# Two fused layers on one Trainium2 core: weight pieces loaded early, shared blocks nearer to their tiles, routing cut into steps

## The chip, the cores and the metric

The kernel runs on one core of one Trainium2 chip. The time is the device time of one execution in microseconds (us); lower is better. In the profile PE is TensorE (PEld its weight loads), DVE is VectorE, ACT is ScalarE, POOL is GpSimd and SP is SyncE, which here only issues DMAs.

## What is computed

The input `x` is 2048 rows (4 batches of 512) of 512 channels. There are two layers, each `x = x + ffn(cond(x))`:

- `cond` gates x with a two-way exponential scan over time. Per batch and channel, with decay d, it runs a = a*d + exp(k)*v and b = b*d + exp(k) forwards and backwards; the output is sigmoid(x) * num / den, scaled per batch. k and v are the side input, so the scans do not depend on x.
- `ffn` of layer 0: an rms norm, then 8 experts (512 to 256 to 512 with silu(g)*u), the 2 best for each row, plus one shared expert for all rows.
- `ffn` of layer 1: 32 experts (512 to 352 to 512), the 6 best for each row with softmax weights, plus a shared expert of width 704, which the kernel treats as two experts of 352.

```
x = x + ffn0(cond0(x));  x = x + ffn1(cond1(x))
y[t] = sum over the top k experts e of w[t,e] * (silu(x W1[e]) * (x W3[e])) W2[e];  plus the shared expert
```

## The kernel before

The rows are cut into 16 tiles of 128. Work for the experts is done in *blocks* of 128 rows by one expert. Blocks are numbered through: 0 to 15 are shared blocks of layer 0, 16 to 54 (`R0` = 16, 39 blocks) routed blocks of layer 0, 55 to 86 (`S1` = 55) the 32 shared blocks of layer 1 (two per tile, experts 32 and 33), and 87 to 214 (`R1` = 87, 128 blocks) its routed blocks. A routed block first gathers its rows by an indirect DMA.

A block has these steps. `gu_pe` (L1749) multiplies the tile by gate and up weights: in layer 1, 24 matmuls, since each weight and each x is held as a high and a low float16 half. `gu` is a tanh on ACT (L1187) and two products on DVE (L1574, L1576). `h_turn` transposes on PE (L1766), ACT copies (L1200), DVE makes the low half (L1584). `down` (L1798) is the second product.

**Weights.** They come as `PIECES` of 128 x 1088 float32 (544 KB) in layer 1, four per expert; pieces 27 to 30 are shared expert 32, 31 to 34 expert 33, 35 to 50 experts 0 to 3. A piece goes through one of two staging buffers `ST`: `w_load` (SP, L923) loads it, `w_hi` (ACT, L1168, and L1172 for pieces whose low half is made by POOL) makes the high half, `w_lo` (DVE L1555 or POOL L975) the low half. A load waits until the low half of the piece two before it is made. `AHEAD` names pieces that are loaded to free parts of the weight buffers and so need no staging buffer; the others are the `RING`.

**Order of the work.** The generator `stages()` yields (step, number) pairs. Every engine walks the same list and takes the steps it has a part in, so the list is the order of each engine's queue, and of SP's and POOL's too. Waits are on semaphores.

**Around the change.** The layer 0 routed loop runs over `j` from 0 to 41; block R0+j starts in step j and ends in step j+3. Its 27 spare steps also carry halves of the scans (`k_...`, DVE L1285 to L1321). Then come two `pick`s (POOL, L1035: each gathers two sets of rows of layer 0's expert output), four splits of weights (`weights(4, 51)`), `x_sum` (DVE, L1341) and a tanh. Then a loop over `s` from 0 to 17 prepares tile s of layer 1: `gate` (DVE, L1332), `f_hi` (ACT, L1131), `f_lo` (DVE, L1358), `row` and `x_turn` (SP: a store, and a DMA transpose, L907), `f_turn` and `logit` (PE L1640 and L1651, ACT L1138, DVE L1370) of the tile before, and `x_sum`, tanh of the tile after. `f_hi` of a tile waits until the transpose of the tile before has landed. Each s has two half steps (slots) `slot = 2s + h`, and each slot runs one shared block:

```
for h in (0, 1):
    b = 2 * (s - 3) + h
    slot = 2 * s + h
```

so the blocks of tile s run at s + 3. At the end of each s one weight piece (two while s < 4) is loaded and split.

**Routing** of layer 1 goes by groups of four tiles (g = 0 to 3). At s = 4g+4, h = 1: `r_top` (DVE: `max` and `max_index` of four tiles L1384 and L1385, L1387, L1392, the one-hot L1393, the sum L1398) and `r_red` (L1404, L1408 or L1410). At s = 4g+5, h = 1: `r_pos` (PE, L1670 to L1674), `r_copy` (DVE L1439), `r_wts` (L1416 to L1431) and `r_slot` (L1445 to L1454, with `split_slot` L1457 to L1461). Then the 24 `hot` steps (DVE L1471, L1475, with PE L1685), six per group. After s = 17 a tail written by hand holds hots 18 to 23, shared blocks 30 and 31, `table1` (L1484, L1486), the first gathers (L1003), and the routed blocks follow.

Of the kernel before, what the change touches and what calls it, by code (L numbers as in the profile page):

```python
# [11 lines left out]
F32 = mybir.dt.float32  # L12
# [80 lines left out]

AHEAD = (17, 18, 19, 20)
RING = [k for k in range(len(PIECES)) if k not in AHEAD]


# [15 lines left out]
def stages():  # L115
# [276 lines left out]
    for j in range(NB0 + 3):  # L392
        n = R0 + j
        if n + 3 < S1:
            yield "gather", n + 3
        if n + 2 < S1:
            yield "x_turn", n + 2
        if n < S1:
            yield "gu_pe", n
        yield from turn_made()  # L400
        if j * 27 // 39 != (j - 1) * 27 // 39 or j >= 39:
            yield from next_half()
        if n - 1 < S1:
            yield "h_turn", n - 1
        if n < S1:
            yield "gu", n
        yield from after_half()
        if n - 2 < S1:
            yield "h_low", n - 2
        if 1 <= j:  # L410
            yield "down", n - 3
        if 37 <= j < 41:
            yield "y_load", j - 37
    while half[0] < 64:
        yield from next_half()
        yield from after_half()
    yield from turn_made()
    for i in range(2):
        yield "pick", i
    yield from weights(4, 51)  # L420
    yield "x_sum", 0
    yield "f_tanh", NT

# [5 lines left out]
    for s in range(18):  # L429
        f = NT + s  # L430
        if 1 <= s <= NT:
            yield "f_turn", f - 1
        if s < NT:
            yield "gate", f
            yield "f_hi", f
            yield "f_lo", f
            yield "row", f
            yield "x_turn", S1 + s
        if s + 2 < NT:
            yield "pick", s + 2  # L440
        if s < 8:
            yield "k_back", s + 8
        for h in (0, 1):
            b = 2 * (s - 3) + h
            slot = 2 * s + h
            yield from shared(b, "gu_pe")
            yield from shared(b - 1, "h_turn")
            yield from shared(b, "gu")
            if h == 1 and s % 4 == 1 and s > 1:
                yield "r_pos", 4 + s // 4 - 1  # L450
                yield "r_copy", 4 + s // 4 - 1
            elif h == 1 and 1 <= s <= NT:
                yield "logit", f - 1
            for g in range(3):
                if 0 <= slot - 1 - 2 * (4 * g + 6) < 6:
                    yield "hot_pe", 6 * g + slot - 1 - 2 * (4 * g + 6)
            yield from shared(b - 2, "down")
            if h == 1 and s % 4 == 1 and 1 < s <= NT:
                yield "logit", f - 1
            if h == 0 and 4 <= s + 2 < NT:  # L460
                yield "y_load", s + 2
            if h == 1 and s + 1 < NT:
                yield "x_sum", s + 1
                yield "f_tanh", f + 1
            for g in range(4):
                if h == 1 and s == 4 * g + 4:
                    yield "r_top", 4 + g
                    yield "r_red", 4 + g
                if h == 1 and s == 4 * g + 5:
                    yield "r_wts", 4 + g  # L470
                    yield "r_slot", g
                if g < 3 and 0 <= slot - 2 * (4 * g + 6) < 6:
                    yield "hot", 6 * g + slot - 2 * (4 * g + 6)
        yield from weights(2 if s < 4 else 1, 51)

    for q in range(18, 21):
        yield "hot", q
# [68 lines left out]
def build(nc, xtok, fT, cst, svec, cond, rout, gatew, W0, W1, Y1):  # L546
    with ExitStack() as ctx:
# [111 lines left out]
        d_pick = [sem(f"d_pick{i}") for i in range(2)]  # L659
        d_first = sem("d_first")  # L660
        d_w = [sem(f"d_w{i}") for i in range(2)]
        d_ahead = sem("d_ahead")
        d_g = [sem(f"d_g{i}") for i in range(3)]
        d_t = [sem(f"d_t{i}") for i in range(4)]
        d_row = [sem(f"d_row{i}") for i in range(6)]
# [55 lines left out]
        def staged(k):  # L721

            l, e, c0, cw, at, who = PIECES[k]
            if k in AHEAD:
                m = AHEAD.index(k)
                to = 18432 + 3072 * (m // 2)
                return (Whi, Wlo)[m % 2][:, to:to + 2 * cw].bitcast(F32), d_ahead, 16 * (m + 1)
            m = RING.index(k)
            return ST[m % 2][:, 0:cw], d_w[m % 2], 16 * (m // 2 + 1)

# [104 lines left out]
        def _(eng):  # L835
# [82 lines left out]
            def w_load(k):  # L918
                l, e, c0, cw, at, who = PIECES[k]
                if k not in AHEAD and k >= 2:  # L920
                    eng.wait_ge(*low(RING[RING.index(k) - 2]))
                at, there, count = staged(k)
                S.dma_start(at, WD[l][e][:, c0:c0 + cw]).then_inc(there, 16)  # L923

# [121 lines left out]
        def _(eng):  # L1046
# [101 lines left out]
            def w_hi_(k):  # L1148
# [3 lines left out]
                eng.wait_ge(there, count)  # L1152
                if k == 21:

                    for j in AHEAD[-2:]:
                        eng.wait_ge(*low(j))
                if spare(k) is not None:
                    eng.wait_ge(b_down, spare(k) + 1)
# [73 lines left out]
        def _(eng):  # L1232
# [128 lines left out]
            def logit(f):  # L1361
                l, i = tile(f)
                E = EXPERTS[l]
                eng.wait_ge(f_lgm, f + 1)
                if l == 0:

                    eng.wait_ge(f_pow, f + 1)
                    V.tensor_scalar(lg[:, i % 4, 0:E], l_bank[l][:, 0:E], sm[:, f, 2:3], None, ALU.mult).then_inc(f_lg, 1)
                else:
                    V.tensor_copy(lg[:, i % 4, 0:E], l_bank[l][:, 0:E]).then_inc(f_lg, 1)  # L1370

            def choices(l, b):

# [4 lines left out]
            def r_top(g):  # L1378
# [1 line left out]
                E, K_ = EXPERTS[l], TOPK[l]  # L1380
                o, ot = choices(l, b)
                eng.wait_ge(f_lg, 4 * g + 4)
                for q in range(4):
                    after(V.max(mx[:, q, :], lg[:, q, 0:E]))  # L1384
                    after(V.max_index(ix[:, q, :], mx[:, q, :], lg[:, q, 0:E]))  # L1385
                m0 = mx[:, :, 0:1]
                op = V.tensor_tensor(ex[:, :, 0:E], lg[:, :, 0:E], bc(m0, [P, 4, E]), ALU.subtract)  # L1387
                if l == 1:
# [1 line left out]
                if l == 0:  # L1390
                    V.tensor_tensor(et[:, :, 0:K_], mx[:, :, 0:K_], bc(m0, [P, 4, K_]), ALU.subtract).then_inc(r_sub, 1)
                after(V.tensor_copy(ixf[:, :, 0:K_], ix[:, :, 0:K_]))  # L1392
                after(V.tensor_tensor(o, bc(iota[:, 0:E].unsqueeze(1).unsqueeze(1), [P, 4, K_, E]),  # L1393
                                      bc(ixf[:, :, 0:K_].unsqueeze(3), [P, 4, K_, E]), ALU.is_equal))

                if g >= 1:
                    eng.wait_ge(r_pos, g)
# [43 lines left out]
            def r_slot(b):  # L1441
# [4 lines left out]
                                                [P, 4, K_, E]), ALU.mult))  # L1446
                ks = slice(0, 4 * K_)
                after(V.tensor_reduce(gq[:, ks].rearrange("p (q k) -> p q k", q=4), ot, AX_X, ALU.add))
                split_slot(ks)
                after(V.scalar_tensor_tensor(out=ja[:, ks].rearrange("p (q k) -> p q k", q=4), in0=ixf[:, :, 0:K_],  # L1450
                                             scalar=4.0, in1=gj[:, ks].rearrange("p (q k) -> p q k", q=4),
# [11 lines left out]
            def hots(h):  # L1463
# [3 lines left out]
                    eng.wait_ge(r_tab, 1 + h - 1)  # L1467
                else:
                    eng.wait_ge(b_down, S1)
                n0 = 4 * h % 24  # L1470
                V.tensor_tensor(A16, bc(iota16[:, :].unsqueeze(1), [P, 4, P]),  # L1471
                                bc(qa[:, n0:n0 + 4].unsqueeze(2), [P, 4, P]), ALU.is_equal)
# [113 lines left out]
            def down(n):  # L1586
                what, l, j = kind(n)
                o, first, last = finished(n)
                if what == "routed" or l == 0 or not last:
# [5 lines left out]
                                       op0=ALU.mult, op1=ALU.add).then_inc(b_outv, 1)  # L1595

            mine = dict(setup=setup, k_min=k_min_, k_fwd=k_fwd, k_bwd=k_bwd, k_den=k_den_, k_rec=k_rec_,
                        k_out=k_out_, x_sum=x_sum, gate=gate, f_var=f_var_, f_lo=f_lo_, logit=logit, r_top=r_top, r_red=r_red_,
                        r_wts=r_wts, r_copy=r_copy, r_slot=r_slot, hot=hot, places0=places0, table0=table0, table1=table1, w_lo=w_lo, weight=weight, gu=gu,
                        h_turn=h_turn, down=down)  # L1600
            for what, n in stages():
                if what in mine:
# [263 lines left out]
```

## Time and profile before

| | us |
|---|---|
| median of 3 runs | 1608.49 (1602.04 to 1611.96) |
| profiled execution, its own time | 1601.73 |
| its span | 1599.6 |
| PE busy | 1342.6 (84%) |
| DVE busy | 1006.1 (63%) |
| ACT, POOL busy | 742.2, 604.6 |

Times within the profile are counted from the start of the span. Busy times are of instructions; PE's matmuls are pipelined, so their single durations overlap. PEclk is the clock granted to TensorE as a share of full speed. In a timeline row, the bracket gives how long the engine was idle before the row and what ended that.

### The profile page before, as it was taken

What the parts mean: (1) busy time and instruction counts of PE and PEld (TensorE: products, weight loads), DVE (VectorE), ACT (ScalarE), POOL (GpSimd) and SP (SyncE); (2) the same over time, 40 slices, a digit from 0 to 9 for tenths busy, and PEclk for the clock granted to TensorE, in tenths of its full rate; (3) what the DMA queues carried; (4) which work ended last, traced back from release to release, by engine and by line L of the source; (5) the groups of instructions that cost most, each with busy time, mean ns of one, the idle gap of its engine ahead of it and who ended that gap; (6) DMA issues with size and microseconds to landing.
All of it is one profiled execution on the core that took longest, in us unless ns stands there. A gap on an engine that the chain in (4) does not pass through costs nothing.

```text
span 1599.6 us, 23683 instructions
## 1 busy us (share of the span) xinstructions
PE 1342.6 (84%) x8220; PEld 811.3 (51%) x8220; DVE 1006.1 (63%) x1748; ACT 742.2 (46%) x1262; POOL 604.6 (38%) x466
## 2 busy tenths in 40 slices
PE   0146666699997289889899999999999999999998
PEld 0023342244443156556565666666666666666664
DVE  8999978979896468888735444444444444444222
ACT  4466664545454543333146454454444445444332
POOL 2344432544431443231033443444444444444443
PEclk9987766899999599999999999999999999999999
DMA  3557644689985896563048988889998988988664
GB/s 101 174 174 187 156 112 92 151 182 195 206 177 159 227 205 145 141 146 83 25 137 233 203 199 212 196 207 199 207 208 195 206 203 204 200 206 184 109 115 74
DMA packets 225234, 269.38 MB, mean 168 GB/s; under 512 B 149664, under 2 KB 149792, under 8 KB 224992
## 3 DMA queue, kind: packets, MB, share of 16 engines
q1 hardware_dynamic: 188464, 175.84, 42.6%
q0 software_dynamic: 36656, 92.03, 29.2%
q8 instruction: 70, 1.15, 0.3%
q14 instruction: 44, 0.36, 0.1%
HBM read 167.87 MB, written 70.32 MB: 149 GB/s over the span
## 4 chain that ended last, share of the span: by engine, by line
PE 60%; DVE 26%; issue 5%; DMA 4%; ACT 3%; POOL 1%; SPq 0%; POOLq 0%; ACTq 0%; DVEq 0%
PE psG L1749 33%; PE psO L1798 19%; DVE wkFD L1314 5%; PE psH L1766 3%; DMA ST<-W 2%; DVE wkFN L1289 2%; DVE wkFD L1296 2%; PE psX L1710 2%; DVE wkFD L1285 2%; DMA XSp<-XG 2%; DVE wkFN L1321 1%; DVE wkFD L1306 1%; DVE H L1574 1%; DVE Wlo L1555 1%; DVE wkFN L1299 1%
## 5 line engine op out<-in xcount | busy, mean ns | idle before, releaser
L1749 PE MATMUL psG<-Whi,XSp 128*128 128x352 f16 (+2 forms) x3000 | 671.8, 329 | 12.1 <-issue 10.8
L1749 PEld LDWEIGHTS psG<-Whi,XSp 128*128 128x128 f16 x3000 | 295.7, 100 | 212.5 <-issue 38.4
L1798 PE MATMUL psO<-Whi,HS 128*128 128x512 f16 (+1 forms) x1180 | 394.5, 387 | 0.0
L1749 PE MATMUL psG<-Wlo,XSp 128*128 128x352 f16 (+2 forms) x1500 | 389.2, 329 | 0.0
L1021 POOL DMA_INDIRECT out<-OB,posb x128 | 202.7, 1583 | 416.1 <-ACT OB L1222 407.5
L1555 DVE SCALAR_TENSOR_TENSOR Wlo<-ST,Whi 128x1088 f16<-128x1088 f32 (+1 forms) x118 | 152.3, 1291 | 235.4 <-ACT Whi L1168 231.4
L1574 DVE SCALAR_TENSOR_TENSOR H<-H,psG 128x352 f32<-128x352 f32 (+1 forms) x215 | 105.5, 491 | 242.2 <-ACT H L1187 221.4
L1798 PE MATMUL psO<-Wlo,HS 128*128 128x512 f16 (+1 forms) x590 | 228.4, 387 | 0.0
L1187 ACT ACTIVATE H<-psG 128x352 f32<-128x352 f32 (+1 forms) x215 | 95.2, 443 | 229.7 <-PE psG L1749 222.5
L1749 PEld LDWEIGHTS psG<-Wlo,XSp 128*128 128x128 f16 x1500 | 149.1, 99 | 93.4 <-issue 8.3
L1798 PEld LDWEIGHTS psO<-Whi,HS 128*128 128x128 f16 x1180 | 117.6, 100 | 120.4 <-issue 9.8
L1222 ACT ACTIVATE OB<-psO,WSL 128x512 f32<-128x512 f32 x128 | 88.1, 688 | 173.7 <-PE psO L1798 173.7
L1003 POOL DMA_INDIRECT XG<-xrows,posb x128 | 129.5, 1012 | 90.9 <-DVE posb L1486 42.4
L1168 ACT ACTIVATE Whi<-ST 128x1088 f16<-128x1088 f32 (+1 forms) x118 | 129.7, 1100 | 28.1 <-DMA ST<-W 28.1
L975 POOL TENSOR_TENSOR Wlo<-ST,Whi 128x1088 f16<-128x1088 f32 (+1 forms) x37 | 82.0, 2218 | 154.6 <-ACT Whi L1172 154.5
L1576 DVE SCALAR_TENSOR_TENSOR H<-H,psG 128x352 f32<-128x352 f32 (+1 forms) x215 | 106.4, 495 | 7.4
L1200 ACT CAST HS<-psH 128x384 f16<-128x384 f32 x160 | 75.7, 473 | 71.9 <-PE psH L1766 71.9
L963 POOL TENSOR_TENSOR wkFN<-wkFN,wkEU 128x512 f32<-128x512 f32 x32 | 40.5, 1267 | 180.6 <-DVE wkEK L1276 169.5
L1314 DVE RECIPROCAL wkFD<-wkFD 128x512 f32<-128x512 f32 x32 | 107.1, 3346 | 0.0
L1620 PE MATMUL psX<-C,wkFN 128*128 128x128 f32 x64 | 16.7, 412 | 101.9 <-DVE wkFN L1321 101.9
L1584 DVE TENSOR_TENSOR HS<-psH,HS 128x384 f16<-128x384 f32 x160 | 88.1, 551 | 16.2 <-ACT HS L1200 16.2
L1766 PE MATMUL psH<-C,H 128*128 128x128 f32 x480 | 80.5, 277 | 19.3 <-DVE H L1576 19.3
(216 smaller groups left out, 1536.9 us busy)
## 6 DMA issues: line engine op xcount, KB each, us to landing
ST<-W SPq DMA_DIRECT2D x136, 544.0 KB
ST<-W SPq DMA_DIRECT2D x23, 512.0 KB
slots<-OB SPq DMA_DIRECT2D x39, 256.0 KB
wkK<-fT SPq DMA_DIRECT2D x32, 256.0 KB
xrows<-XG SPq DMA_DIRECT2D x20, 256.0 KB, 4.4
y0rows<-x SPq DMA_DIRECT2D x8, 512.0 KB, 5.5
y0rows<-OB POOLq DMA_DIRECT2D x16, 256.0 KB, 4.3
out<-OB SPq DMA_DIRECT2D x16, 256.0 KB
```

Source lines behind the costliest of these rows:

```text
L1003: G.indirect_dma_start(out=XG[g % 3][:, 0:w], out_offset=None, in_=X[l][:, :], in_offset=bass.IndirectOffsetOnAxis(ap=idx[l][:, j:j + 1], ...
L1021: G.indirect_dma_start(out=Y1[:, :], out_offset=bass.IndirectOffsetOnAxis(ap=idx[1][:, j:j + 1], axis=0), in_=OB[o % 4][:, :], in_offset=N ...
L1168: op = A.activation(st if who == "pool" else hi, st, ACT.Copy, scale=WS)
L1187: A.activation(H32[a][:, 0:F], psG[a][0][:, 0:F], ACT.Tanh, scale=0.5 * UN).then_inc(b_tanh, 1)
L1222: A.activation(OB[o % 4][:, :], psO[bank(o)][:, :], ACT.Copy, scale=scale).then_inc(b_outa, 1)
L1314: V.reciprocal(FD[n % 2][:, :], FD[n % 2][:, :]).then_inc(k_rec, 1)
L1555: op = V.scalar_tensor_tensor(out=Wlo[:, at:at + cw], in0=st, scalar=WS, in1=Whi[:, at:at + cw], op0=ALU.mult, op1=ALU.subtract)
L1574: V.scalar_tensor_tensor(out=H, in0=H, scalar=1.0, in1=g, op0=ALU.add, op1=ALU.mult).then_inc(b_sil, 1)
L1576: V.scalar_tensor_tensor(out=H, in0=H, scalar=(-0.5, 0.5)[l] * XS * UN * UN, in1=u, op0=ALU.mult, op1=ALU.mult).then_inc(b_h, 1)
L1749: op = M.matmul(o, hx[:, x, q * P:q * P + P], w(half_, off + c, nn), start=first, stop=last)
L1766: op = M.transpose(bank_[:, q * P:q * P + P], H32[a][:, q * P:q * P + P], ident)
L1798: op = M.matmul(psO[bank(o)][:, :], hs(n)[:, x, q * P:q * P + P], columns[n](half_, off0 + q * 512, 512), start=(q == 0 and x == 0 and hal ...
```

## The change

It has three parts. (1) Pieces 29 and 30 join `AHEAD`; pieces 27 and 28 are loaded to the two staging buffers at j = 20 of the layer 0 routed loop, 29 and 30 at j = 22 and 24, to bytes of the weight buffers that the layer 0 shared expert had. After the loop come the four `y_load`s (moved there from j = 37 to 40), the splits of 27 and 28, the two picks, the loads of 31 and 32, and the splits of 29 and 30. Each piece in `AHEAD` has a semaphore of its own. (2) A shared block b runs in slot b + 4 instead of b + 6, for b up to 27; blocks 28 and 29 run in slots 33 and 35, where 32 and 34 have none. The tail is unchanged. (3) Layer 1's routing: `max` and `max_index` of each tile directly after its logits; the sum over the one-hot (`r_mask`) and `r_red` half a stage later; `r_wts` and the second part of `r_slot` (`r_place`) half a stage after the first part.

```
-AHEAD = (17, 18, 19, 20)
+AHEAD = (17, 18, 19, 20, 29, 30)
...
-        if 37 <= j < 41:
-            yield "y_load", j - 37
+        if j == 20:
+            yield from loads(2, 51)
+        if j in (22, 24):
+            yield "w_load", 29 + (j - 22) // 2
...
     yield from turn_made()
+    for i in range(4):
+        yield "y_load", i
+    yield from splits(2)
     for i in range(2):
         yield "pick", i
-    yield from weights(4, 51)
+    yield from loads(2, 51)
+    yield from splits(2)
...
-            b = 2 * (s - 3) + h
             slot = 2 * s + h
+            b = slot - 4 if slot < 32 else {33: 28, 35: 29}.get(slot, -9)
...
                 if h == 1 and s == 4 * g + 4:
                     yield "r_top", 4 + g
+                if h == 0 and s == 4 * g + 5:
+                    yield "r_mask", 4 + g
                     yield "r_red", 4 + g
                 if h == 1 and s == 4 * g + 5:
+                    yield "r_slot", g
+                if h == 0 and s == 4 * g + 6:
                     yield "r_wts", 4 + g
-                    yield "r_slot", g
+                    yield "r_place", g
...
+    yield "r_wts", 7
+    yield "r_place", 3
...
             def w_load(k):
...
+                if k in AHEAD and l == 1:
+
+                    eng.wait_ge(b_down, R0)
...
             def logit(f):
...
+                    eng.wait_ge(f_lg, f + 1)
+                    largest(i % 4, E)
+
+            def largest(q, E):
+                after(V.max(mx[:, q, :], lg[:, q, 0:E]))
+                after(V.max_index(ix[:, q, :], mx[:, q, :], lg[:, q, 0:E]))
...
+            def r_place(b):
+                K_ = TOPK[1]
+                ks = slice(0, 4 * K_)
                 split_slot(ks)
```

The first hots and the high half of piece 47 also wait for the low halves of pieces 29 and 30, whose staging bytes they overwrite.

## Rows read from the trace of the kernel before

**Rows 1.** Busy time by stretch: us, then each engine's busy time, PEclk, DMA share, GB/s.
```profile
556.10:591.90 35.80, 33.65 (x207) 21.41 (x205) 20.90 (x42) 18.13 (x26) 15.51 (x9) 0.93 0.97 206
...
556.10:807.40 251.30, 224.98 (x1483) 143.63 (x1481) 188.05 (x429) 84.11 (x141) 64.35 (x42) 0.96 0.52 126
...
591.90:653.70 61.80, 56.32 (x375) 36.30 (x372) 49.97 (x111) 21.80 (x37) 18.11 (x13) 0.97 0.65 153
653.70:715.30 61.60, 55.58 (x374) 36.16 (x374) 49.99 (x111) 21.79 (x37) 18.14 (x13) 0.97 0.57 140
715.30:777.00 61.70, 56.28 (x391) 36.81 (x392) 46.67 (x109) 19.21 (x35) 9.20 (x6) 0.97 0.26 76
777.00:807.40 30.40, 23.16 (x141) 12.96 (x140) 20.52 (x61) 3.18 (x6) 3.39 (x4) 0.89 0.17 54
...
890.00:1600.00 710.00, 701.77 (x4612) 439.24 (x4610) 305.47 (x555) 323.72 (x501) 299.99 (x230) 1.00 0.84 185
```
**Rows 2.** Who PE waited for, 556 to 815: us in total, times, longest.
```profile
PE psH L1766 <- DVE H L1576: 19.3, 9, 4.2
```
**Rows 3.** DVE's timeline in two groups: start us, us, engine, line, instruction.
```profile
584.73 0.19 DVE L1384 MAX8 mx<-lg 128x8 f32<-128x32 f32 x1
...
586.83 0.29 DVE L1387 TENSOR_TENSOR ex<-lg,mx 128x128 f32<-128x128 f32 x1
...
588.24 1.51 DVE L1398 TENSOR_REDUCE mask<-OH 128x128 f16<-128x768 f32 x1
...
590.19 1.76 DVE L1408 COPY macc<-mred 128x32 f16<-128x32 f16 x1
591.87 0.68 DVE L1332 SCALAR_TENSOR_TENSOR XR<-XR,RT 128x512 f32<-128x512 f32 x1
...
602.12 0.28 DVE L1416 TENSOR_REDUCE s<-ex 128x4 f32<-128x128 f32 x1
...
605.16 2.20 DVE L1457 CAST gi<-gq 128x24 int32<-128x24 f32 x1
...
608.68 0.69 DVE L1332 SCALAR_TENSOR_TENSOR XG<-XG,RT 128x512 f32<-128x512 f32 x1
```
**Rows 4.** DVE's timeline, the gates of tiles 7, 8 and 9.
```profile
619.77 0.68 DVE L1332 SCALAR_TENSOR_TENSOR XG<-XG,RT 128x512 f32<-128x512 f32 x1
...
633.17 0.68 DVE L1332 SCALAR_TENSOR_TENSOR XR<-XR,RT 128x512 f32<-128x512 f32 x1
...
653.72 0.68 DVE L1332 SCALAR_TENSOR_TENSOR XR<-XR,RT 128x512 f32<-128x512 f32 x1
```
**Rows 5.** Timeline of all engines between the layers, 512 to 557.
```profile
512.93 0.60 ACT L1222 ACTIVATE OB<-psO 128x512 f32<-128x512 f32 x1 [0.70 <-PE psO L1798]
...
517.98 0.97 POOL L1035 DMA_INDIRECT wkFD<-slots,sl  x1 [14.76 <-DMA slots<-OB]
...
519.50 1.11 ACT L1168 ACTIVATE Whi<-ST 128x1088 f16<-128x1088 f32 x1 [5.97 <-DMA ST<-W]
...
523.18 2.24 POOL L975 TENSOR_TENSOR Wlo<-ST,Whi 128x1088 f16<-128x1088 f32 x1 [0.43 <-ACT Whi L1172]
...
531.87 2.30 DVE L1332 SCALAR_TENSOR_TENSOR XG<-XG,RT 128x512 f32<-128x512 f32 x1 [1.99 <-ACT XG L1108]
...
543.87 1.09 PE L1640 MATMUL psX<-C,XG 128*128 128x128 f32 x4 [0.62 <-issue]
...
556.11 0.80 PE L1749 MATMUL psG<-Whi,XSp 128*128 128x352 f16 x2
```
**Rows 6.** The picks (L1035), 505 to 760: from issue to landing.
```profile
DMA to landing us min/median/max: 3.5/5.4/10.6
```
**Rows 7.** The chain of waits, 440 to 900: start us, us, what.
```profile
514.39 6.45 DMA ST<-W
```
**Rows 8.** The layer 0 routed loop, 340 to 505: busy by stretch.
```profile
340.00:505.00 165.00, 154.56 (x767) 75.98 (x765) 147.70 (x174) 87.20 (x198) 61.73 (x54) 1.00 0.84 188
```
**Rows 9.** The layer 0 routed loop: who waited for whom.
```profile
PE psG L1749 <- DMA XSp<-XG: 0.7, 1, 0.7
```

More of the change, by code:

```diff
@@ L661, in build @@
         d_w = [sem(f"d_w{i}") for i in range(2)]
-        d_ahead = sem("d_ahead")
+        d_ahead = [sem(f"d_ahead{i}") for i in range(6)]
         d_g = [sem(f"d_g{i}") for i in range(3)]
@@ L726, in staged @@
                 to = 18432 + 3072 * (m // 2)
-                return (Whi, Wlo)[m % 2][:, to:to + 2 * cw].bitcast(F32), d_ahead, 16 * (m + 1)
+                return (Whi, Wlo)[m % 2][:, to:to + 2 * cw].bitcast(F32), d_ahead[m], 16
             m = RING.index(k)
@@ L1153, in w_hi_ @@
                 if k == 21:
-                    for j in AHEAD[-2:]:
+                    for j in AHEAD[2:4]:
+                        eng.wait_ge(*low(j))
+                if k == 27 + 4 * 5:
+                    for j in AHEAD[4:]:
                         eng.wait_ge(*low(j))
@@ L1382, in r_top @@
                 eng.wait_ge(f_lg, 4 * g + 4)
-                for q in range(4):
-                    after(V.max(mx[:, q, :], lg[:, q, 0:E]))
-                    after(V.max_index(ix[:, q, :], mx[:, q, :], lg[:, q, 0:E]))
+                if l == 0:
+                    for q in range(4):
+                        largest(q, E)
                 m0 = mx[:, :, 0:1]
@@ L1394, in r_top, with r_mask_ @@
                                       bc(ixf[:, :, 0:K_].unsqueeze(3), [P, 4, K_, E]), ALU.is_equal))
+                if l == 0:
+                    r_mask_(g)
+            def r_mask_(g):
+                l, b = divmod(g, 4)
+                E = EXPERTS[l]
+                o, ot = choices(l, b)
                 if g >= 1:
@@ L1469, in hots @@
                     eng.wait_ge(b_down, S1)
+                    for j in AHEAD[4:]:
+                        eng.wait_ge(*low(j))
                 n0 = 4 * h % 24
@@ L1597, in _ @@
             mine = dict(setup=setup, k_min=k_min_, k_fwd=k_fwd, k_bwd=k_bwd, k_den=k_den_, k_rec=k_rec_,
-                        k_out=k_out_, x_sum=x_sum, gate=gate, f_var=f_var_, f_lo=f_lo_, logit=logit, r_top=r_top, r_red=r_red_,
-                        r_wts=r_wts, r_copy=r_copy, r_slot=r_slot, hot=hot, places0=places0, table0=table0, table1=table1, w_lo=w_lo, weight=weight, gu=gu,
+                        k_out=k_out_, x_sum=x_sum, gate=gate, f_var=f_var_, f_lo=f_lo_, logit=logit, r_top=r_top, r_red=r_red_, r_mask=r_mask_,
+                        r_wts=r_wts, r_copy=r_copy, r_slot=r_slot, r_place=r_place, hot=hot, places0=places0, table0=table0, table1=table1, w_lo=w_lo, weight=weight, gu=gu,
                         h_turn=h_turn, down=down)
```

## The prediction

> **What bounds the kernel now.** I read the busy time by stretch first, then PE's waits, then the timelines of single engines. From 890 us to the end PE is busy 701.8 of 710 us at full clock [rows 1]: the routed blocks of layer 1 run at PE's pace, and the change does not touch them. So whatever is won before 807.40, when the first routed block starts, should come through to the end unchanged, unless the weight loads behind it depend on the clock time; they don't, they are issued in the order of the list.
>
> The change acts on three places. (a) Between the layers: the last output of layer 0 is made at 512.93 and the first shared block of layer 1 starts at 556.11 [rows 5]; in these 43 us PE does little. (b) The shared stage, 556.10 to 807.40: PE is busy 225.0 of 251.3 us, so 26.3 are idle: 2.2 up to 591.9, then 5.5, 6.0 and 5.4 in three groups of about 61.7, and 7.2 in the tail [rows 1]. 19.3 us of waits on this stage are one kind: PE's transpose waiting for DVE's product [rows 2]. (c) The layer 0 routed loop, into which loads are put: PE busy 154.6 and DVE 147.7 of 165 us, the DMA engines 84% [rows 8].
>
> Why PE waits for DVE is seen in DVE's timeline. At the end of one stage in four DVE does `r_top` and `r_red` in one go from 584.73 to 591.87, 7.1 us, and one stage later `r_wts` and `r_slot` from 602.12 to 608.68, 6.6 us [rows 3]. Behind them in its queue stand the gate, the low half and the products of the next block. A stage without them takes 633.17 - 619.77 = 13.4 us, the one that ends in `r_top` 653.72 - 633.17 = 20.55 [rows 4]. The granted clock falls with it: 0.97 over each group [rows 1].
>
> **Part 1, loads ahead and splits first.** Now ACT ends the last output at 512.93 + 0.60 = 513.5 and starts splitting piece 27 at 519.50, since its load was only issued then; the gate of tile 0 runs from 531.87 to 534.17, 2.30 long where others take 0.68 [rows 4, 5]. After the change pieces 27 and 28 lie in their buffers, so by ACT durations of 1.11 us:
> - ACT: 27 to 514.7, 28 (two passes) to 516.9; POOL's low half, 2.24 [rows 5], to 519.2.
> - POOL's queue: the picks now stand behind that low half and start at 519.2 instead of 517.98. So the edit costs the picks 1.2. The second gather of pick 0 is issued 1.3 later, 520.5, and lands 5.4 later (median, 3.5 to 10.6) [rows 6]: 525.9.
> - DVE: two sums of 0.75 (L1341), tanh 0.6 (ACT L1108), gate 0.7: the gate ends at about 528.7, against 534.17. That is 5.5 earlier. DVE no longer has the low half of 29 ahead of `x_sum`, and the gate does not meet POOL's low half.
>
> The `y_load`s go from inside the loop to behind the last store on SP, some 2 us of issues that land before the picks: nothing. From the gate on, the steps of tiles 0 and 1 are the same and in the same order, with the same loads beside them (eight pieces split before s = 2 in both), so PE's transpose of tile 1 goes from 543.87 [rows 5] to about 538.4.
>
> **Part 2, blocks two slots earlier.** `gu_pe` of the first shared block now stands right behind that transpose (1.1 us): 539.5 instead of 556.11, 16.6 earlier. Its weights 27 to 30 are split long before. Block 1 needs piece 34, whose low half is the last of s = 1, about 546; block 0 at the low clock takes 6 to 7 us, so PE waits about 1. At s = 2 and 3 ACT still has two pieces per stage to split ahead of the tanh of a block, and PE, which had no blocks at s = 2, will now wait there once, about 2. The low clock at the start costs as before plus about 2.5, since PE did less before. Start-up extra: 5.5.
>
> **Part 3, routing in steps.** The work stays: DVE is busy 50.0 of 61.8 us in a group [rows 1], which includes all of it. What goes is the block of 7.1 and that of 6.6. They become, per slot: 0.53 per tile after its logits, 1.4 (L1387 to L1393), 2.1 to 3.6 (L1398 to L1408), 1.9 (L1445, L1448), 1.1 + 3.5 (`r_wts`, `r_place`) [rows 3]. A slot of PE is 6.7 us; DVE's own work in one is 3.8 to 4.1 and a hot 1.5. So the worst slots have 5.6 + 1.5 = 7.1 and 5.3 + 4.6 = 9.9, against 6.7 and a slack of about 3, the time that PE spends on `down` and the next `gu_pe` before it needs the products. Nearly all of it fits: I leave 1.5 us of idle per group instead of 5.5 to 6.0, and give back 1.2 per group for the clock. Bounds: nothing left (0) and nothing won (5.6).
>
> The row L1408 copies 32 columns in 1.76 us, as the cast L1457 of 24 columns takes 2.20 [rows 3]; each ends with a POOL low half that it met. The Trainium skill (SBUF — State Buffer, "SBUF: two separate sides") says that DVE and GpSimd share a port pair by an exclusive lock that is held for the whole instruction. By that rule cutting the routing into steps cannot remove these meetings, only move them. The trace agrees, and the 1.1 us (L1408) and 2.0 us (L1457) are kept in the slots above.
>
> **The loads in the layer 0 loop.** Four pieces more. Lower bound nothing: in 165 us PE waited 0.7 us for a transpose [rows 9], and one is issued two blocks before its use. Upper bound: the whole time to the landing of a piece in a crowd, 6.45 [rows 7], for each of four: 26. Nearest is the slack row, so 1. PE and DVE are both near full here, so nothing is gained either. The Trainium skill (DMA: Bandwidth & Descriptors, "Queues, rings and completion order") says that each DMA engine takes the descriptors of one ring in order. By this a transpose issued by SP just after the pieces waits for them, which speaks against the change; no row here shows such a pair. It would take the cost from 1 towards the upper bound, and is the rival below.
>
> **The sum.** 539.5 + PE's work 225.0 - 3 x 1.2 (clock) + idle outside the groups 2.2 + 7.2 + groups 3 x 1.5 + start-up 5.5 = 780.3, against 807.4: 27.1. The tail: the last group's routing chain (logit 31 to `r_place`) now has blocks 28 and 29 over it instead of 26 to 29. Counted through from the logits it needs about 13.4 us to hot 18 while PE has 18 of work to the end of block 31, so it is covered; I allow 1.1. Minus 1 for the loop: gain 25. Span 1574.6, own time 1576.7. The profiled execution lies 6.8 below the median of the three runs (1608.49); against that median, 1583.5. I forecast 1583.5 us.
>
> **The rivals.**
> - *DVE becomes the bound of the shared stage.* DVE would be busy 50 of some 56 us, and the slot with `r_wts`, `r_place`, a hot and a POOL meeting is over budget. If the groups keep 4 to 5.5 of idle and the low clock, 8 to 15 of the gain go: 1592 to 1600, middle 1594. For it: the 9.9 us slot. Against: the stages with hots alone run at 13.4, with PE full.
> - *The start moves, not the blocks.* The first block is early, but then waits: picks that land after 10.6 [rows 6] and transposes that hold `f_hi` up, so that only the 5.5 and part of the 11 remain. Gain 16 to 18: 1591. Against: from s = 2 on the tiles have 13 us per stage, and need 8.
> - *More than forecast.* Nothing remains of the groups' idle and the start costs nothing extra: 4.5 + 4 + 1.1 more, gain 35: 1573.
> - *Slower: transposes behind the pieces in the layer 0 loop.* Place: j = 20 to 24. If each piece holds a transpose back past its slack, DVE, which carries the scans there, and PE both stop, up to 26 [rows 7]; with the next gather, that waits for the transpose, doubling it, up to 40 or more. It decides from 25 us, over 6 per piece: 1608 to 1625, at its middle 1612. Against: the 0.7 us of rows 9.
> - *That the change does nothing* would need the first block to start where it did; it stands two slots earlier in PE's list and its weights are there, so 2 in 100.
>
> **How the numbers follow.** A measurement of this kernel tells about 1%, 16 us, from no change. Forecast (gain 18 to 32) 0.60; DVE bound 0.15; start only 0.09; more than forecast 0.08; slower 0.05; nothing 0.03. Faster by over 1%: forecast, more, a fifth of the DVE case and over half of the start case, 0.60 + 0.08 + 0.04 + 0.06 = 0.78. Slower by over 1%: part of its case and unknowns, 0.04. Within 1%: 0.18. The range takes in gains of 12 to 38: 1570 to 1597.
>
> **What would show it.** Right: the first PE row of L1749 in layer 1 near 539 to 541 and a first routed block near 782; the gate of tile 0 at 0.7 us; stages of 13.4 to 14.5 us throughout, PE idle under 2 in each group and PEclk 0.99 or 1.00 there; PE's wait for L1576 under 8 us instead of 19.3; the stretch from the first routed block to the end unchanged at 792. Wrong: a last layer 0 output later than 515 (the loads hurt), PE in the groups waiting for L1576 in the slot after `r_place`, or gates still 15 us apart.

## The result, and the profile after

| | kernel before | changed kernel |
|---|---|---|
| median, us | 1603.95 (1600.6 to 1611.96, 20 runs) | 1599.03 (1594.6 to 1602.0, 20 runs) |
| profiled execution: own time, span | 1601.73, 1599.6 | 1600.68, 1598.8 |
| first shared block, first routed block of layer 1 | 556.11, 807.40 | 541.69, 804.94 |

The ratio is 0.9963 [0.9951, 0.9975]: 5 to 6 us faster (the medians are 4.9 apart), where 25 were forecast (1583.5, range 1570 to 1597). The gain is clear of noise and under 1%. The forecast's ratio against its own median was 0.984. That median, 1608.49 of 3 runs, lies 4.5 above the one of 20 runs here, so the gain misses its forecast by some 20 us, while the time misses it by 15.5 only.

The busy time by stretch of the changed kernel: the shared stage, its start, its three groups, its tail, the routed blocks. The columns are those of [rows 1].

```profile
541.70:804.90 263.20, 231.83 (x1493) 147.18 (x1492) 188.69 (x433) 88.23 (x147) 68.47 (x46) 0.94 0.59 131
541.70:592.70 51.00, 44.46 (x253) 27.70 (x252) 25.80 (x50) 22.21 (x34) 18.52 (x12) 0.87 0.86 194
592.70:651.80 59.10, 55.45 (x382) 36.68 (x381) 48.54 (x111) 22.02 (x38) 17.73 (x12) 1.00 0.77 168
651.80:710.70 58.90, 54.35 (x376) 35.72 (x375) 48.74 (x111) 21.71 (x38) 17.70 (x12) 1.00 0.71 147
710.70:771.00 60.30, 50.92 (x315) 31.72 (x313) 43.10 (x101) 18.26 (x32) 11.17 (x6) 0.89 0.31 72
771.00:804.90 33.90, 26.65 (x175) 15.37 (x174) 22.51 (x64) 4.03 (x8) 3.35 (x4) 0.90 0.16 48
890.00:1598.00 708.00, 700.44 (x4602) 438.16 (x4600) 305.40 (x555) 323.77 (x501) 299.44 (x230) 1.00 0.85 185
```

The shared stage starts 14.4 us earlier and is 11.9 longer (263.2 against 251.3), so 2.5 remain at the first routed block. From there to the end it is 793.9 us, against 792.2. Over all the profiles of this case that stretch takes 792.2 to 795.0, so the end carries through what is won before it, as assumed, but only to within some 3 us. The three groups are 59.1, 58.9 and 60.3 long instead of 61.7, 6.8 us less together, where the prediction's three groups of 1.5 idle and a 1.2 repayment for the clock stood for about 16. (The third group isn't the same work: the shift leaves it 315 matmuls instead of 391.)

Who PE waited for, 537 to 815, in the changed kernel (us in total, times, longest):

```profile
PE psO L1724 <- DVE Whi L1514: 7.9, 5, 2.1
PE psH L1805 <- DVE H L1615: 7.9, 6, 2.2
PE psX L1690 <- ACT HT L1154: 6.0, 1, 6.0
PE psO L1724 <- DVE Wlo L1514: 5.9, 3, 3.4
PE psX L1709 <- DVE mask L1430: 4.2, 3, 1.5
```

The 19.3 us for H [rows 2] are 7.9. But PE now waits 13.8 us for the selectors of `hot` (L1514; 3.1 in the kernel before) and 4.2 for the mask, for which it did not wait before. Between the layers and at the start of the stage (timeline of the changed kernel; start us, us, engine, line, instruction, idle before it and its releaser):

```profile
514.31 0.60 ACT L1241 ACTIVATE OB<-psO 128x512 f32<-128x512 f32 x1 [0.70 <-PE psO L1837]
514.80 1.10 ACT L1187 ACTIVATE Whi<-ST 128x1088 f16<-128x1088 f32 x1
...
520.50 1.85 POOL L1051 DMA_INDIRECT wkFD<-slots,sl  x1
...
526.12 2.26 POOL L991 TENSOR_TENSOR Wlo<-Wlo,Whi 128x1088 f16<-128x1088 f32 x1
526.37 2.57 DVE L1360 SCALAR_TENSOR_TENSOR wkK<-wkFD,wk,wkK 128x512 f32<-128x512 f32 x1 [4.86 <-DMA wkFN<-slots,sl]
528.97 0.75 DVE L1360 SCALAR_TENSOR_TENSOR wkK<-wkFN,wk,wkK 128x512 f32<-128x512 f32 x1
...
530.41 0.69 DVE L1351 SCALAR_TENSOR_TENSOR XG<-XG,RT 128x512 f32<-128x512 f32 x1 [0.70 <-ACT XG L1124]
...
541.69 0.79 PE L1788 MATMUL psG<-Whi,XSp 128*128 128x352 f16 x2
...
549.07 0.46 PE L1788 MATMUL psG<-Whi,XSp 128*128 128x352 f16 x2 [1.92 <-POOL Wlo L991]
```

Against [rows 5]: ACT splits piece 27 right behind the last output, the first gate ends at 531.10 instead of 534.17, and the first shared block stands right behind the transpose of tile 1. The stages, from gate to gate of tiles 0 to 15 (each the difference of two such L1332 or L1351 rows), show where the time went again:

```
before   8.0 8.2  9.1 13.4 21.2 16.8 11.1 13.4 20.6 16.7 11.0 13.4 20.5 16.6 11.0   sum 211.1
changed  6.4 8.9 14.1 15.9 17.0 15.5 15.4 13.4 14.8 15.3 15.3 13.4 14.8 16.9 16.7   sum 213.8
```

The stages of tiles 2 and 3, which now hold the early blocks, went from 22.5 to 30.0 us; and at the other end, slot 32 holds no `gu_pe` any more, so PE has nothing between the last `down` and the selectors of `hot`:

```profile
754.77 2.11 DVE Wlo L1510
...
757.83 0.61 PE L1724 MATMUL psO<-Wlo 128*128 128x128 f16 x4 [3.41 <-DVE Wlo L1514]
...
758.23 0.79 PE L1788 MATMUL psG<-Whi,XSp 128*128 128x352 f16 x2
...
764.17 0.46 PE L1788 MATMUL psG<-Whi,XSp 128*128 128x352 f16 x2
```

(The first line is of the chain of waits, the others of the timeline.) PE waits 3.41 us and comes back at 0.79 us for a pair of matmuls instead of 0.46, the lower of its two levels, for most of block 28.

### The profile page after: what moved, and what is told of

Its sections match the earlier page's. It is cut to its first block, busy times and chain, and to the rows that moved or that the text cites. A ratio compares the mean times of both kernels' runs of the same rounds, so it can differ in the third digit from the quotient of the medians.

```text
span 1598.8 us, 23690 instructions
## 1 busy us (share of the span) xinstructions
PE 1345.1 (84%) x8220; PEld 811.5 (51%) x8220; DVE 1003.3 (63%) x1748; ACT 740.8 (46%) x1262; POOL 602.0 (38%) x466
## 4 chain that ended last, share of the span: by engine, by line
PE 59%; DVE 25%; issue 7%; ACT 4%; DMA 4%; POOL 1%; SPq 0%; POOLq 0%; ACTq 0%; DVEq 0%
PE psG L1788 33%; PE psO L1837 19%; DVE wkFD L1333 5%; PE psH L1805 3%; DMA ST<-W 2%; DVE wkFN L1308 2%; DVE wkFD L1304 2%; PE psX L1749 2%; DVE wkFD L1315 2%; DMA XSp<-XG 1%; DVE wkFN L1340 1%; DVE wkFD L1325 1%; DVE H L1613 1%; DVE XG L1377 1%; DVE Wlo L1594 1%
## 5 line engine op out<-in xcount | busy, mean ns | idle before, releaser
L1659 PE MATMUL psX<-C,wkFN 128*128 128x128 f32 x64 | 16.6, 411 | 101.5 <-DVE wkFN L1340 101.5
L1623 DVE TENSOR_TENSOR HS<-psH,HS 128x384 f16<-128x384 f32 x160 | 88.1, 550 | 15.5 <-ACT HS L1219 14.9
```

## The experiments

The expectations name their theories by letters, and A does not mean the same in all of them. For `only_loads` and `only_steps`, A is the prediction's sum taken part by part. For `only_shift`, A says that an earlier first block counts (10 to 12 us), and C that the shift only lengthens the stages it enters and leaves the emptied slots slow (0 to 4 us). In `late_shift`, what C said is called A. Theory D, on record with the first runs and tested by the later ones, says that cutting up the bursts turns PE's waits for H into waits for `hot` and the mask. All ratios are to the kernel before, run on the same chip beside them.

**The parts alone.** `only_loads` is the kernel before with the early loads and splits (the `AHEAD`, `loads`, `splits` and `w_load` edits), `only_steps` with the step routing (`r_mask`, `r_place`, `largest`), and `only_shift` with one line (and a separate semaphore for each `AHEAD` piece, as in the changed kernel):

```diff
-            b = 2 * (s - 3) + h
             slot = 2 * s + h
+            b = slot - 4 if slot < 32 else {33: 28, 35: 29}.get(slot, -9)
```

`only_loads`. Expected:

> Part 1 alone (pieces 27 to 30 loaded ahead, splits before the picks, y_loads after the loop); blocks and routing as before. Theory A (each part gives what the sum said, the loss is in the others): the start gains its 3 to 5 us and all of it comes through to the end: 1600 us, 3 to 4 below the kernel before. Theory B (the loads cost the layer 0 loop what they give the start): within 2 us of the kernel before; the last layer 0 output is 1.4 us later in the trace.

`only_shift`. Expected:

> Part 2 alone (shared blocks two slots earlier, none in slots 32 and 34). Theory A (PE is the bound of the shared stage, so an earlier first block counts): 10 to 12 us faster. Theory C (the stage is paced by DVE's and ACT's queue, tile by tile, so blocks that are two slots nearer only make the stage s = 2 longer and leave PE idle and slow in the empty slots): 0 to 4 us faster, the gate of the last tile 4 to 6 us later than before, PE waiting for the hots at slot 32.

`only_steps`. Expected:

> Part 3 alone (routing in steps). Theory A: PE's waits for DVE's products go from 19 us to under 8 and nothing takes their place: 13 to 16 us faster. Theory D (the wait moves: PE's hot_pe waits for the hot that now stands behind r_wts and r_place, and r_pos for the mask): 4 to 8 us faster, with 5 us or more of PE waits on the hots (L1471/L1475 by the old numbers) and 3 us on the mask.

`no_steps`, the loads and the shift together. Expected:

> Parts 1 and 2 without part 3. If the parts add up, this lies above the changed kernel by what only_steps gains. Theory A: 13 to 16 us above it, 1613. Theory C and D: 4 to 8 us above it, 1603 to 1607, that is about the kernel before.

| kernel | median, us | ratio |
|---|---|---|
| only_loads | 1600.16 | 0.9964 [0.9947, 0.9982] |
| only_shift | 1610.27 | 1.0022 [0.9998, 1.0045] |
| only_steps | 1600.18 | 0.9969 [0.9954, 0.9985] |
| no_steps (loads and shift) | 1605.47 | 0.9997 [0.9979, 1.0014] |

The loads are worth 0.36% and the steps 0.31%, each by an interval clear of 1. That is what A forecast for the loads, though their profile has the last layer 0 output 2.3 us later (515.20). For the steps it is D's 4 to 8 us, not A's 13 to 16. The shift alone is not faster, and added to the loads it undoes them (0.9997 against 0.9964; C and D had put `no_steps` at 1603 to 1607). The profile of `only_shift` has the first block at 545.22, 10.9 us earlier, and the first routed block at 808.55, 1.1 later. The stages of tiles 2 and 3 are 13.1 and 14.9 instead of 9.1 and 13.4, the sum to the last gate is 217.3 instead of 211.1, and the rest from there is 58.9 instead of 64.5: 6.2 lost, 5.6 won. That is nearest to theory C, which still gave 0 to 4 us of gain and a last gate 4 to 6 us later (it is 6.7 later); the 10 to 12 us of its rival are not there. In `only_steps` alone the waits on the selectors are there too, without the shift and the loads, so they belong to the steps:

```profile
PE psO L1712 <- DVE Whi L1502: 8.0, 5, 2.1
PE psH L1793 <- DVE H L1603: 6.4, 6, 2.2
...
PE psX L1697 <- DVE mask L1421: 4.4, 3, 1.5
```

**The changed kernel without the shift, and two trials on it.** `no_shift` undoes the one line above. `shift_full` fills the emptied slots instead, and has none in 34 and 35:

```diff
-            b = slot - 4 if slot < 32 else {33: 28, 35: 29}.get(slot, -9)
+            b = slot - 4 if slot < 34 else -9
```

`late_pe` is `no_shift` with PE's matmuls that need DVE's routing put behind the `down` of the slot, so that 1.9 us of PE's own work cover the wait:

```diff
-            if h == 1 and s % 4 == 1 and s > 1:
-                yield "r_pos", 4 + s // 4 - 1
-                yield "r_copy", 4 + s // 4 - 1
...
-                    yield "hot_pe", 6 * g + slot - 1 - 2 * (4 * g + 6)
             yield from shared(b - 2, "down")
+            if h == 1 and s % 4 == 1 and s > 1:
+                yield "r_pos", 4 + s // 4 - 1
+                yield "r_copy", 4 + s // 4 - 1
...
+                    yield "hot_pe", 6 * g + slot - 1 - 2 * (4 * g + 6)
```

`quiet_loads` is `no_shift` with the four loads at the end of the layer 0 loop:

```diff
-        if j == 20:
+        if j == 36:
             yield from loads(2, 51)
-        if j in (22, 24):
-            yield "w_load", 29 + (j - 22) // 2
+        if j in (37, 38):
+            yield "w_load", 29 + j - 37
```

Expected of `no_shift`:

> Parts 1 and 3 without the shift of the blocks. If the parts add: only_loads gave 0.36% and only_steps 0.31%, the shift cost 0 to 0.2%; so 0.6 to 0.7% faster than before, about 1593 to 1595, and faster than the changed kernel by 4 us. If the shift has a gain that needs the steps beside it (theory A for part 2), it is not faster than the changed kernel (0.37%).

Of `shift_full`:

> The changed kernel with blocks 28 and 29 in slots 32 and 33, and none in 34 and 35. Theory C has two halves: the start (s = 2 and 3 longer by some 5.5 us) and the end (slots without a block leave PE waiting and slow). If the empty slots 32 and 34 are the trouble, this is 2 to 4 us faster than the changed kernel; if the end is set by the last group's routing chain on DVE whatever PE has, it is within 2 us of it.

Of `late_pe`:

> As no_shift, with PE's hot_pe and r_pos (and DVE's r_copy) put behind the down of their slot instead of ahead of it. Theory D (the steps' gain was turned into PE's waits for the hots and the mask, 13 us in the trace of only_steps): these waits fall under 4 us, PE's busy share in the groups rises, and the time is 6 to 10 us below no_shift. Rival E (DVE's queue paces the stages, so PE only waits elsewhere): within 2 us of no_shift, with more waits for DVE's products.

Of `quiet_loads`:

> As no_shift, with the four loads at j = 36 to 38 instead of 20 to 24, where the DMA engines are busy 13 to 44% instead of 84%. If the loads hurt the layer 0 loop by holding transposes back (the last layer 0 output came 1.2 to 2.3 us later), the last output is back at 513 and the time 1 to 2 us below no_shift. If not, the last output stays near 514 to 515 and the time is that of no_shift.

| kernel | median, us | ratio |
|---|---|---|
| no_shift | 1598.27 | 0.9949 [0.9929, 0.9969] |
| shift_full | 1598.10 | 0.9954 [0.9935, 0.9973] |
| late_pe | 1590.96 | 0.9908 [0.9884, 0.9932] |
| quiet_loads | 1594.07 | 0.9929 [0.9905, 0.9954] |

`no_shift` is not slower than the changed kernel, though its first block starts later (550.07). It missed the 1593 to 1595 that adding the two parts gave; its interval holds both that sum (0.9933) and the changed kernel's 0.9963, so whether the loads and the steps add in full is open. `shift_full` lies between the two, within the 2 us of the changed kernel that its expectation gave for an end set by something else: filling slots 32 and 33 does not rescue the shift. Its waits for L1514 are 11.5 us instead of 13.8, and those for the mask 7.4 instead of 4.2. In `late_pe` most of the waits of theory D go, at the price of one new one. First `no_shift`, then `late_pe`, who PE waited for from 537 to 815:

```profile
PE psO L1724 <- DVE Whi L1514: 7.7, 4, 2.1
PE psH L1805 <- DVE H L1615: 6.7, 6, 2.2
...
PE psX L1709 <- DVE mask L1430: 4.4, 3, 1.5
PE psO L1724 <- DVE Wlo L1514: 1.5, 1, 1.5
```

```profile
PE psH L1805 <- DVE H L1615: 5.2, 5, 2.2
PE psX L1690 <- DVE le L1471: 4.6, 3, 1.6
PE psO L1724 <- DVE Whi L1514: 1.9, 3, 1.5
...
PE psO L1724 <- DVE Wlo L1514: 1.1, 1, 1.1
```

13.6 us of waits on `hot` and mask became 3.0, with 4.6 new ones for `le` (the logit behind `r_copy` waits for it), a net 6.0. The medians are 7.3 us apart, though the two intervals still touch; the executions profiled here are no help in this, since that of `no_shift` was its fastest (1589.7) and that of `late_pe` its slowest (1593.5). The busy time by stretch of `late_pe` over its three groups:

```profile
592.00:651.00 59.00, 55.72 (x381) 36.27 (x378) 49.33 (x113) 21.63 (x37) 18.37 (x13) 1.00 0.78 161
651.00:711.00 60.00, 55.94 (x382) 36.41 (x383) 50.34 (x113) 22.46 (x39) 18.69 (x13) 1.00 0.73 152
711.00:770.00 59.00, 55.84 (x395) 36.41 (x394) 45.43 (x109) 17.03 (x30) 6.76 (x3) 1.00 0.31 70
```

PE at full clock is busy 55.8 us in a group of four stages, and its chain of waits from 734 to 767 us consists of PE's own instructions. In this order of the work that is the floor of a group, and not four stages of 13.4.

**The last four.** `late_quiet` is `late_pe` with the loads of `quiet_loads`; `late_shift` is the changed kernel, shift included, with the late place; `late_alone` is the kernel before with the late place and nothing else; `hot_late` is `no_shift` with `hot_pe` late but `r_pos` and `r_copy` where they were:

```diff
             yield from shared(b - 2, "down")
+            for g in range(3):
+                if 0 <= slot - 1 - 2 * (4 * g + 6) < 6:
+                    yield "hot_pe", 6 * g + slot - 1 - 2 * (4 * g + 6)
```

> Parts 1 and 3, the shared blocks in their old slots, TensorE's selector matmuls (hot_pe, r_pos) behind the slot's down matmuls, and the three early loads issued at j = 36 to 38 instead of 20 to 24. If the two savings are of different things (the held transpose in the loop of the first layer, 3 to 4 us; TensorE's waits on VectorE's selectors, 7 us), they add: ratio 0.986 to 0.990, last first-layer output at 512 to 513.5. If the quiet loads' gain was spread between executions only, the ratio is late_pe's, 0.991, within 0.001.

> The changed kernel whole (all three parts), with hot_pe and r_pos behind the down matmuls. Theory A (the shift buys nothing because the stages are paced by VectorE, ScalarE and the transfers' chains tile by tile, and the emptied slots give back what the start took): still not below late_pe's 0.991; ratio 0.990 to 0.994. Rival B (the shift was hidden only by TensorE's waits on the selectors): with those gone it shows its worth, 8 us or more below late_pe, ratio under 0.986.

> The kernel before with nothing but hot_pe and r_pos behind the down matmuls. Its TensorE waits are for H (19.3 us) behind long routing bursts on VectorE, which this does not shorten, and the down matmuls would wait no less. Theory D (the late place removes waits that the spread routing made): 0 to 3 us, ratio 0.998 to 1.000. Rival (the late place pays whatever VectorE does): 7 us, ratio 0.9955.

> Parts 1 and 3 with hot_pe alone behind the down matmuls; r_pos and r_copy stay ahead of them. TensorE's waits for the selectors of hot (9.2 us in no_shift) go to 3, those for the mask (4.4) stay, and the 4.6 us for le of late_pe do not appear. If both moves cancel in r_pos, the ratio is late_pe's 0.991 within 0.001; if r_pos's place paid too, it is 0.993.

| kernel | median, us | ratio |
|---|---|---|
| late_quiet | 1591.01 | 0.9907 [0.9884, 0.9929] |
| late_shift | 1592.93 | 0.9920 [0.9898, 0.9942] |
| late_alone | 1606.93 | 1.0011 [0.9994, 1.0028] |
| hot_late | 1592.80 | 0.9925 [0.9902, 0.9947] |

- `late_shift`: with the late place the shift still wins nothing. In the profiles its first gate to its last takes 206.7 us against 200.9 in `late_pe` (tiles 2 and 3: 13.8 and 14.9 against 9.2 and 13.8), and the rest to the first routed block 60.8 against 64.4. Lost 5.8, won 3.7. Its rival, 8 us or more, is out for the shift as it is written. But not all waits were gone: PE still waits 6.3 us for the low selectors, at the emptied slots, where `late_pe` waits 1.1. Blocks 28 and 29 in slots 32 and 33 together with the late place were not tried. The low clock is not what lengthens the stages of tiles 2 and 3, since here they run at full clock and are long all the same. The wait, and the busy time by stretch from the start of tile 2's stage (the two stages end at 574.0):

```profile
PE psO L1724 <- DVE Wlo L1514: 6.3, 3, 3.4
```

```profile
545.30:579.00 33.70, 27.73 (x181) 17.86 (x179) 14.76 (x30) 16.20 (x24) 13.58 (x9) 1.00 0.78 187
```

- `late_alone`: the late place pays only behind the step routing, as theory D has it. It was expected at 0.998 to 1.000 and came to 1.0011, with 1 inside its interval. The wait for H is still 16.5 us.
- `hot_late`: of the 0.41% between `no_shift` and `late_pe`, `hot_pe` alone brings 0.24. Whether `r_pos` adds the rest is within the intervals. The wait for the mask stays at 4.4 us and none for `le` appears, as expected.
- `late_quiet`: no faster than `late_pe`, so the two savings do not add, and the 4 us of `quiet_loads` are most likely spread between executions. By this pair, `quiet_loads` and `late_quiet`, the late place is worth 0.22%; it is 0.41% from `no_shift` to `late_pe` and 0.43% from the changed kernel to `late_shift`: 3.5 to 7 us. The last layer 0 output was at 512.2 in the profiles of both `no_shift` and `quiet_loads`, at 517.1 in that of `late_pe` and at 513.4 in that of `late_quiet`. Over all profiles it is at 512.2 to 517.1 with the loads at j = 20 to 24 (eight kernels), and at 511.4 to 513.5 with none or late ones (six). So the early loads may cost the loop 1 to 2 us; it is not settled beyond that.

## Why the prediction was wrong, step by step

Right: the loads ahead bring the first gate forward; the gate takes 0.69; the routing bursts go and PE's wait for H falls under 8; PEclk is 1.00 in the first two groups; the tail idles 7.2 (7.25, but over a stretch with 175 matmuls instead of 141, so the match is in part luck); the routed blocks are untouched. The sum ended at 780.3 and the first routed block came at 804.94. The 24.6 us are in three of its terms:

- *First block 539.5:* it came at 541.7, 2.2 late. The last layer 0 output was 1.4 later than before, and `x_sum` took 2.57 us beside POOL's low half of 526.12 instead of 0.75: the prediction had seen that the gate no longer meets a low half, and not that the sum ahead of it now does. The gate ended 3.1 us earlier, not 5.5. The mechanism was right, and its size off.
- *PE's work 225.0 less 3.6 for the clock:* PE was busy 231.8, 10.4 more. At the start the clock is 0.87 over 51 us (0.93 in [rows 1]), and the last group has 0.89, where the sum counted on full clock. The work was taken as a fixed sum that could be moved for nothing.
- *Idle 19.4 in all:* 31.4 was measured, 12.0 more. The start has 6.5 (7.7 was given, but 2.5 of it for the low clock, which is work and not idle time) and the tail 7.25; the groups have 3.65, 4.55 and 9.38 instead of 1.5 each. So all of the excess lies in the groups.

By parts, the forecast gain of 25 us was 4.5 for the loads (5.5 less 1 for the loop), 4.5 for the shift (16.6 - 5.5 - 5.5 - 1.1) and 16.0 for the steps (5.5 + 6.0 + 5.4 less 3 x 1.5, and 3 x 1.2 for the clock). Measured, each as the difference between a kernel with the part and the same one without it, the loads give 0.20 to 0.36% (3 to 6 us, as forecast), the steps 0.15 to 0.34% (2.5 to 5.5 us), and the shift takes 0.12 to 0.33% (2 to 5 us). So the larger loss is in the steps, some 10 to 13 us, and the shift's is 6 to 10.

Some small slips in the prediction's numbers change nothing here: the middles of 1592 to 1600 and of 1608 to 1625 are 1596 and 1616.5, not 1594 and 1612, and "nothing" has 2 in 100 in one place and 0.03 in another.

**The first step that failed is "blocks two slots earlier, 16.6 us".** Treating PE's work as a sum that starts earlier makes every block moved forward a gain. It would be, if PE's work were all that the stages consist of. But the stage of a tile runs through its gate, its transpose and its routing, and the loop has the same number of stages whatever the blocks do. Two blocks in tile 2's stage make it 13.1 to 14.1 us in the five kernels with the shift, instead of 8.2 to 10.1, and tile 3's is longer too. At the other end two blocks leave the tail: one costs PE 3.58 us of `gu_pe`, 0.33 of `h_turn` and 1.94 of `down` in the chain of waits, so two are some 12 us (an estimate from these rows). But the time from the last gate to the first routed block falls by only 3.7 to 5.6 us, while first gate to last grows by 5.7 to 6.2, in three pairs of profiles with and without the shift. (The fourth pair has 2.5 and 10.8, against the fastest execution of `no_shift`.) In the tail, PE waits at the emptied slots for DVE's `hot`. That the last group's chain of `hot` steps sets the end whatever PE holds is argued from this and from `shift_full`, where filling the slots left 59.7 us of 60.7; it is not shown by itself.

The rival "the start moves, not the blocks" was near, with a start of 14.4 us forward. It named late picks and transposes that hold `f_hi` up behind the first block: the second came (4.84 us against 3.42, see the last section), but is too small to be the loss, and the rival left 16 to 18 us. The sum's sentence "it is covered; I allow 1.1" is the same fault seen from the other end: emptying slots 32 and 34 cost waits of 3.41 and 1.42 us for `hot` and a block at the low clock (0.77 from 757.60 to 771.00). That was a count of DVE's chain to hot 18 against all of PE's work to the end of block 31, and not slot by slot. Four pairs with and without the shift show it as worth nothing, or a little less: 1.0022 against 1, 0.9997 against 0.9964, 0.9963 against 0.9949, 0.9920 against 0.9908. Each pair's intervals touch, and all four have the same sign.

**The second, and the larger, is "nearly all of it fits: I leave 1.5 us of idle per group".** DVE's busy time per slot was compared with PE's slot and a slack of 3 us for H, and the other things that PE takes from DVE in the slot, `hot_pe` and `r_pos`, were left out. They had next to none: the timeline of DVE in the changed kernel has `r_place` and the two selectors one after the other, and PE at the far end. Of the 13.8 us for the selectors, 4 to 5 belong to the slots that the shift emptied (`no_shift` has 9.2).

```profile
615.66 0.18 DVE L1490 TENSOR_TENSOR qa<-qa,gj 128x24 f32<-128x24 f32 x1
615.87 0.69 DVE L1510 TENSOR_TENSOR Whi<-iota,qa 128x512 f16<-128x512 f16 x1
616.48 0.98 DVE L1514 TENSOR_SCALAR Whi<-iota,ja,C 128x128 f16<-128x128 f16 x4
...
617.61 0.38 PE L1724 MATMUL psO<-Whi 128*128 128x128 f16 x4 [2.13 <-DVE Whi L1514]
```

`late_pe` shows that this is the cause of a part, 3.5 to 7 us by the three pairs above: with 1.9 us of `down` in front, most of the wait is gone and the group is as short as PE's work and 3 to 4 us more. What the rest of the missing 16 us is was not taken apart. The rival "DVE becomes the bound" (1592 to 1600, 0.15) named this slot, and at 1599 the time is inside it; but what remained was a wait on one instruction's place in PE's list, not DVE's busy time: DVE is busy 49 of 59 us in `late_pe` as well.

The rival of a slower loop did not come. PE waited 3.0 us for transposes there, in two waits of 1.22 and 1.81, each behind early pieces, against 0.7 [rows 9], and the pair that no row of before showed is now there (timeline of SP's queue and of PE):

```profile
417.66 0.90 SPq L939 DMA_DIRECT2D ST<-W  x2
...
418.66 2.31 SPq L920 DMA_TRANSPOSE XSp<-XG  x1
...
422.32 0.39 PE L1788 MATMUL psG<-Whi,XSp 128*128 x1 [1.22 <-DMA XSp<-XG]
```

A transpose issued right behind two pieces held PE for 1.22 us. The Trainium skill (DMA: Bandwidth & Descriptors, "Queues, rings and completion order") has each DMA engine work through one ring in order, so the transpose stands behind the pieces. This row agrees, but its price is 1.2 us, where the upper bound of 6.45 per piece would have given 26; and in the profile of `no_shift`, with the same loads in the same places, PE did not wait for a transpose at all.

## What to carry to other kernels

Where an order is written out by stages, count a moved block by what it does to the stage that it enters and to the one that it leaves, and not by PE's total: here the stages grew by about 6 us, and the end, which two blocks of some 12 us had left, shrank by 4 to 6. When the burst in front of a wait is broken up, list all the other things that the same engine takes from it in the same slot, since the next in the list takes the wait's place; moving those behind work that needs nothing new (`down`) was worth 0.22 to 0.43%, as much as any part of the change. The version to use is parts one and three with the late place, 1590.96 us, 0.9908 [0.9884, 0.9932]. It is faster than both kernels, by 0.9% and by some 0.5%.

## What the runs showed that was not expected

The meetings of DVE with POOL's low halves did move, as the prediction had it, but out of the slots it kept them in. The rows are of DVE by line, with their mean in ns, before and then changed:

```profile
L1358 DVE SCALAR_TENSOR_TENSOR XG<-XR,XG 128x512 f16<-128x512 f32 x10 | 12.2, 1222 | 23.3 <-ACT XG L1131 23.3
...
L1457 DVE CAST gi<-gq 128x24 int32<-128x24 f32 x4 | 6.8, 1697 | 0.1
...
L1410 DVE TENSOR_TENSOR macc<-macc,mred 128x32 f16<-128x32 f16 x3 | 3.7, 1235 | 0.1
```

```profile
L1377 DVE SCALAR_TENSOR_TENSOR XG<-XR,XG 128x512 f16<-128x512 f32 x10 | 17.2, 1722 | 27.0 <-ACT XG L1147 27.0
...
L1493 DVE CAST gi<-gq 128x24 int32<-128x24 f32 x4 | 0.7, 170 | 0.0
...
L1442 DVE TENSOR_TENSOR macc<-macc,mred 128x32 f16<-128x32 f16 x3 | 0.5, 175 | 0.1
```

The cast of 24 columns fell from 1.70 us to 0.17, and `f_lo` of 512 columns rose from 1.22 to 1.72. Over the shared stage the instructions that met POOL's low halves (that cast, the copy and the sums of 32 columns, `gate` and `f_lo`) take 44.5 us before and 39.4 after: `f_lo` gained 7.3 and the others lost 12.4. `f_lo` stands behind the gate, where POOL is at the low half of the piece split at the end of the stage before (609.15 for 2.25 us on POOL, 610.12 for 1.84 on DVE). So most of the meetings moved, as the prediction took from the rule of the Trainium skill quoted there (SBUF — State Buffer, "SBUF: two separate sides"), and the rows agree with it; but some 5 us of them went away, which "cannot remove these meetings, only move them" excludes. One more met `x_sum` ahead of this stretch (2.57 us instead of 0.75). The 1.1 and 2.0 us that the prediction kept in the routing slots were not there, and PE waited 2.13 us behind the slot that it called the worst all the same.

The transposes of the shared stage's first tiles take some 10 us to land, as they did before (9.32 and 10.78 us in the chain of waits of the kernel before), and the prediction's sum has no term for them. The first row is of the chain of waits in the changed kernel, the others are ACT's timeline:

```profile
541.19 10.64 DMA XSp<-XG
...
551.93 0.63 ACT L1147 ACTIVATE XG<-XR 128x512 f16<-128x512 f32 x1 [4.84 <-DMA XSp<-XG]
...
552.47 0.45 ACT L1206 ACTIVATE H<-psG 128x352 f32<-128x352 f32 x1
```

`f_hi` needs the buffer that this transpose reads, so ACT stands still for 4.84 us, and the tanh of the first early block stands behind it. The same wait is in the kernel before (553.68, 3.42 us), with no block behind it yet. Without the shift it is 2.6 us in `no_shift` and 3.5 in `late_pe`. This is one thing in which the stage that the blocks entered differs from the one that they left.

Last, executions of one kernel differ by 5 to 15 us here (1588.3 to 1593.5 for `late_pe`, 1589.7 to 1602.8 for `no_shift`), and in single profiles the stages of the last group were 16.6 in one kernel and 18.2 in another with the same instructions. Single profiles were therefore read for waits and places, and the medians of several rounds for what a part is worth.
